# Chunk tables of a graph kernel: every second batch of step matrices on ScalarE, and PE's expansion loop in turns of 16 groups instead of 64

## The reference

```python
def _spmm(row, col, vals, x):
    msg = vals[:, None] * x[col]
    return segment_sum(msg, row, num_segments=N)
def _layer(x_prev, row, col, vals, W_a, b_a, W_b, b_b):
    h = _spmm(row, col, vals, x_prev)
    z = (h + x_prev) @ W_a.T + b_a + h * x_prev @ W_b.T + b_b
    return where(z >= 0, z, 0.2 * z)
x = emb[x_ids]; x1 = _layer(x, ...); x2 = _layer(x1, ...); x3 = _layer(x2, ...)
return concatenate((x, x1, x2, x3), axis=1)
```

## Time and profile before

| | us |
|---|---|
| median of 3 runs (8888.81 to 8897.76) | 8891.55 |
| the profiled execution | 8889.35 |
| its span | 8887.5 |
| mean granted TensorE clock, share of full speed | 0.938 |
| busy PE / PEld / DVE | 7889.6 / 7229.6 / 7142.9 |
| busy ACT / POOL | 4541.7 / 5736.8 |

### The profile page before, as it was taken

How to read it: one execution, slowest core, us unless ns; L and a number is a source line. 1 busy time by engine, 2 the same in 40 slices (tenths; PEclk the granted TensorE clock), 3 DMA queues, 4 the chain that set the end, 5 groups by cost and what they waited for, 6 DMA issues and landing times.

```text
span 8887.5 us, 265258 instructions
## 1 busy us (share of the span) xinstructions
PE 7889.6 (89%) x82756; PEld 7229.6 (81%) x82757; DVE 7142.9 (80%) x9830; ACT 4541.7 (51%) x14097; POOL 5736.8 (65%) x4886
## 2 busy tenths in 40 slices
PE   5999995799996688899999788899999788899999
PEld 4777775577774588789999788899999688799999
DVE  8999988799997877777777777777777777777777
ACT  0999990799995366621112566611112566611112
POOL 4787874588883244478886344478885444488884
PEclk8999995899997799999999899999999899999999
DMA  2111111211111488788887588888886688888885
GB/s 79 7 7 7 7 7 39 34 7 7 7 7 26 159 295 294 289 286 283 286 286 244 204 296 295 302 277 286 286 286 220 228 295 290 296 283 286 286 286 199
DMA packets 877540, 1680.36 MB, mean 189 GB/s; under 512 B 262122, under 2 KB 313399, under 8 KB 876404
## 3 DMA queue, kind: packets, MB, share of 16 engines
q0 software_dynamic: 364832, 907.43, 34.4%
q1 hardware_dynamic: 499692, 758.75, 24.0%
q10 hardware_dynamic: 12520, 6.40, 0.2%
HBM read 912.31 MB, written 759.79 MB: 188 GB/s over the span
## 4 chain that ended last, share of the span: by engine, by line
PE 45%; ACT 19%; issue 12%; DMA 8%; SPq 7%; DVE 5%; POOL 1%; ACTq 1%; DVEq 0%; POOLq 0%
PE ps L1037 35%; ACT hT L723 17%; DMA messages<-work 7%; SPq L684 6%; PE ps L1028 5%; PE ps L864 1%; DVE hT L1348 1%; SPq L669 1%; DVE hT L1134 1%; PE ps L1065 1%; PE ps L1045 1%; PE ps L1066 1%; PE ps L891 1%; POOL work L575 1%; DVE work L1385 1%
## 5 line engine op out<-in xcount | busy, mean ns | idle before, releaser
L1037 PE MATMUL ps<-work 128*128 128x125 f32 x26880 | 3111.5, 278 | 52.6 <-DVE work L1414 52.6
L1037 PEld LDWEIGHTS ps<-work 128*128 128x128 f32 x26880 | 3066.2, 192 | 97.9 <-DVE work L1414 57.4
L603 POOL DMA_INDIRECT work<-messages,work x1680 | 2567.6, 1528 | 557.7 <-issue 550.0
L1028 PE MATMUL ps<-xb,work 125*128 x10752 | 1992.4, 226 | 450.9 <-DVE work L1385 265.8
L792 ACT ACTIVATE work<-ps,work 128x128 f32<-128x128 f32 x5376 | 1526.9, 371 | 1073.4 <-PE ps L1028 572.0
L1414 DVE TENSOR_TENSOR work<-work,iota_p 128x1000 f32<-128x1000 f32 x1680 | 2005.2, 1194 | 1.0 <-ACT work L810 0.4
L1028 PE MATMUL ps<-hT,work 125*128 x10752 | 1991.7, 224 | 0.4
L1028 PE MATMUL ps<-work 125*128 x10752 | 1976.6, 224 | 0.8
L810 ACT ACTIVATE work<-work 128x8 f32<-128x8 f32 x1680 | 516.2, 307 | 2527.8 <-DMA work<-messages,work 2527.8
L917 PEld LDWEIGHTS ps<-hT 128*128 128x128 f32 x12768 | 1484.1, 196 | 297.1 <-ACT stage L712 227.9
L917 PE MATMUL ps<-hT 128*128 128x96 f32 x12768 | 1520.1, 280 | 186.6 <-ACT stage L712 186.5
(11 more groups left out here) (212 smaller groups left out, 6096.0 us busy)
## 6 DMA issues: line engine op xcount, KB each, us to landing
messages<-work SPq DMA_DIRECT2D x2688, 258.0 KB, 4.0
work<-messages,work POOLq DMA_INDIRECT x1680, 5.9
out_x<-xb SPq DMA_DIRECT2D x150, 125.0 KB
sorted_edges<-stage,run_idx POOLq DMA_INDIRECT x798
work<-slot_cols SPq DMA_DIRECT2D x672, 4.0 KB
work<-lane_places SPq DMA_DIRECT2D x532, 5.2 KB, 2.1
out_x<-xb ACTq DMA_DIRECT2D x4, 1562.5 KB
sorted_edges<-hT SPq DMA_DIRECT2D x4, 908.0 KB
```

The costliest lines, as they stand in the source:

```text
L603: pool.indirect_dma_start(out=ck[:, n, :, :].rearrange("p j e -> p (j e)"), out_offset=None, in_=messages, in_offset=bass.IndirectOffsetOn ...
L1028: last = t.matmul(ps[:, n % PR, j * D:(j + 1) * D], col_hot[:, at:at + P], piece[:, bass.ds(offset, D)], start=k == 0, stop=k == 2)
L1037: last = t.matmul(part[n], ck[:, n, j, 0:D], sel[:, n % SELB, j, :], start=j == 0, stop=j == CHB - 1)
```

## The change

Two parts of the kernel are changed, and the rest stands as it was.

In the chunk tables, the batches with odd numbers are made by ScalarE. It takes Sign(x + 0.5 - tt[1]), which is 1 where the comparison is true and -1 where it is not, one tile per instruction. For these tiles the differences are multiplied by 0.5 ahead, and the sum lacks a constant, half of the sum of all differences, which is SLOTS2 / 2 and is added behind the reduction. There are four buffers instead of two, a semaphore for each of the two makers, and one more table, tt[5], with 0.5 - tt[1].

In the expansion, PE's loop does 16 groups per turn, 56 turns in a layer. At the head of a turn it loads 16 bytes into 16 registers; each holds one block number, and there is no shift and no mask.

```diff
-LB = 4
-CQ = 2
+CQ = 4
-        group_at = wi[0:1, TBL0 + 2 * TB:TBL0 + 2 * TB + GROUPS // 4]
-        group_bytes = wu[0:1, 4 * (TBL0 + 2 * TB):4 * (TBL0 + 2 * TB) + GROUPS]
+        group_at = wu[0:1, 4 * (TBL0 + 2 * TB):4 * (TBL0 + 2 * TB) + GROUPS]
...
+            act.wait_ge(vals_kept, GPP)
+            act.wait_ge(starts_ready, 1)
+            for k in range(1, TB // CR, 2):
+                act.wait_ge(cstep_used, k + 1)
+                for n in range(CR):
+                    last = s.activation(chunk_step[:, k % CQ, n, :], iota_p[0:NBD, :], ACT.Sign, bias=tt[5][:, k * CR + n:k * CR + n + 1])
+                last.then_inc(cstep_ready[1], 1)
...
             for k in range(TB // CR):
-                pe.wait_ge(cstep_ready, k + 1)
+                pe.wait_ge(cstep_ready[k % 2], k // 2 + 1)
...
-                with pe.Fori(0, ABODIES // LB) as i:
-                    _, four = nc.values_load_multi_w_load_instructions(
-                        group_at[0:1, bass.ds(i * (LB * AU // 4), LB * AU // 4)], engines=[mybir.EngineType.PE],
-                        min_val=0, max_val=(NB - 1) * 0x01010101,
-                        skip_runtime_bounds_check_because="the table holds four numbers of blocks in each word")
-                    for n in range(LB * AU):
-                        offset = ((four[n // 4] >> (n % 4 * 8)) & 255) * D
-                        offset.max_val = (NB - 1) * D
+                with pe.Fori(0, ABODIES) as i:
+                    _, block_of = nc.values_load_multi_w_load_instructions(
+                        group_at[0:1, bass.ds(i * AU, AU)], engines=[mybir.EngineType.PE],
+                        min_val=0, max_val=NB - 1, skip_runtime_bounds_check_because="the table holds numbers of blocks")
+                    for n in range(AU):
...
-                                                piece[:, bass.ds(offset, D)], start=k == 0, stop=k == 2)
+                                                piece[:, bass.ds(block_of[n] * D, D)], start=k == 0, stop=k == 2)
...
+            signed = delta_t.rearrange("c (b e r) h -> c e b (r h)", e=2, r=CR)[:, 1, :, :]
+            link(v.tensor_scalar(signed, signed, 0.5, None, ALU.mult))
+            v.tensor_scalar(tt[5], tt[1], -1.0, 0.5, ALU.mult, ALU.add).then_inc(starts_ready, 1)
-            for k in range(TB // CR):
+            for k in range(0, TB // CR, 2):
                 dve.wait_ge(cstep_used, k + 1)
                 v.tensor_tensor(chunk_step[:, k % CQ, :, :], iota_p[0:NBD, :][:, None, :].to_broadcast([NBD, CR, P]),
                                 tt[1][:, k * CR:(k + 1) * CR][:, :, None].to_broadcast([NBD, CR, P]),
-                                ALU.is_ge).then_inc(cstep_ready, 1)
+                                ALU.is_ge).then_inc(cstep_ready[0], 1)
...
+            by_sign = chunk_idx.rearrange("p (b e r) -> p e b r", e=2, r=CR)[:, 1, :, :]
+            link(v.tensor_scalar(by_sign, by_sign, SLOTS2 / 2, None, ALU.add))
```

More of the change, by code:

```diff
@@ L263, in graph_layers @@
         base_of = work[:, TBL0 + TB:TBL0 + 2 * TB]
-        group_at = wi[0:1, TBL0 + 2 * TB:TBL0 + 2 * TB + GROUPS // 4]
-        group_bytes = wu[0:1, 4 * (TBL0 + 2 * TB):4 * (TBL0 + 2 * TB) + GROUPS]
-        assert ABODIES % LB == 0 and NB <= 128
+        group_at = wu[0:1, 4 * (TBL0 + 2 * TB):4 * (TBL0 + 2 * TB) + GROUPS]
+        assert 4 * TBL0 % 16 == 0 and TB % 2 == 0 and AU % 16 == 0 and NB <= 256
         row_at = wi[0:1, TBL0 + 2 * TB + GROUPS:TBL0 + 3 * TB + GROUPS]
@@ L283, in graph_layers @@
         TT0 = 18 * NBD + max(TBW, GTW) * NB
-        tt = [hT[0:NBD, TT0 + k * TB:TT0 + (k + 1) * TB] for k in range(5)]
-        TS0 = TT0 + 5 * TB
+        tt = [hT[0:NBD, TT0 + k * TB:TT0 + (k + 1) * TB] for k in range(6)]
+        TS0 = TT0 + 6 * TB
         chunk_step = hb[0:NBD, 2 * TS0:2 * TS0 + CQ * CR * P].rearrange("c (q r x) -> c q r x", q=CQ, r=CR)
         delta_t = hb[0:NBD, 2 * (TS0 + CQ * CR * P // 2):2 * (TS0 + CQ * CR * P // 2) + 3 * TB].rearrange("c (t h) -> c t h", h=3)
-        assert TB // 4 * 3 <= 512 and TB % (4 * CR * CQ) == 0 and TS0 + CQ * CR * P // 2 + 2 * TB <= HSORT
+        assert TB // 4 * 3 <= 512 and TB % (4 * CR) == 0 and TS0 + CQ * CR * P // 2 + 2 * TB <= HSORT
         part = [ps[:, n, 0:BLK] for n in range(BU)]
@@ L354, in graph_layers @@
         tabs_done = sem("tabs_done")
-        cstep_ready = sem("cstep_ready")
+        starts_ready = sem("starts_ready")
+        cstep_ready = [sem(f"cstep_ready{e}") for e in range(2)]
         cstep_used = sem("cstep_used")
@@ L658, in _ @@
             sp.wait_ge(offsets_stored, 3 * DMA)
-            sp.dma_start(group_bytes, group_blocks.rearrange("p t -> (p t)")[0:GROUPS].rearrange("(a t) -> a t", a=1)).then_inc(offsets_in, DMA)
+            sp.dma_start(group_at, group_blocks.rearrange("p t -> (p t)")[0:GROUPS].rearrange("(a t) -> a t", a=1)).then_inc(offsets_in, DMA)
             sp.dma_start(row_at, tile_rows.rearrange("p t -> (p t)")[0:TB].rearrange("(a t) -> a t", a=1)).then_inc(offsets_in, DMA)
@@ L1013, in _ @@
                 pe.sem_inc(pe_layers, 1)
-                with pe.Fori(0, ABODIES // LB) as i:
-                    _, four = nc.values_load_multi_w_load_instructions(
-                        group_at[0:1, bass.ds(i * (LB * AU // 4), LB * AU // 4)], engines=[mybir.EngineType.PE],
-                        min_val=0, max_val=(NB - 1) * 0x01010101,
-                        skip_runtime_bounds_check_because="the table holds four numbers of blocks in each word")
-                    for n in range(LB * AU):
-                        offset = ((four[n // 4] >> (n % 4 * 8)) & 255) * D
-                        offset.max_val = (NB - 1) * D
+                with pe.Fori(0, ABODIES) as i:
[3 more added lines that the diff above has]
+                    for n in range(AU):
                         if n % 2 == 0:
-                            pe.wait_ge(col_hot_ready, la * (GROUPS // 2) + i * (LB * AU // 2) + (n // 2 + 1))
-                        pe.wait_ge(msg_ready[n % 2], la * (GROUPS // 2) + i * (LB * AU // 2) + (n // 2 + 1))
+                            pe.wait_ge(col_hot_ready, la * (GROUPS // 2) + i * (AU // 2) + (n // 2 + 1))
+                        pe.wait_ge(msg_ready[n % 2], la * (GROUPS // 2) + i * (AU // 2) + (n // 2 + 1))
                         for j in range(CH):
```

## The result

The changed kernel takes 9671.81 us (median of 4, 9669.28 to 9674.77) against 8894.65 us (4 runs of the kernel before). The ratio is 1.087, with a 95% interval of 1.085 to 1.089: 777 us slower. The prediction said 8805 us, 8675 to 8890, and gave slower a chance of 0.13. The profiled execution took 9673.08 us with a span of 9671.3.

A forecast was written before the change was run, and what follows sets the result against it. DVE bounds the chunk tables; in the expansion, message stores bound most of a turn and PE the time around each gap. From 8889.35 us, 17.6 (tables) and 67.1 (loop) come off: 8804.6, said as 8805 us, range 8675 to 8890.

The forecast's parts named there:

- The tables: Chunk-table loop: odd batches on ScalarE make it the new bound, 85.4 us against 103.0, a gain of 17.6 us.
- The lower bound of the gain: Chunk tables: worst case, no overlap between ScalarE's activations, 109 us for them, gain put at -9 us.
- The branch: End of a turn of PE's expansion loop: with 384 records the branch falls from 4.19 to 0.21 us.
- the rule of two pages: PE's loop branch: a target outside two 256-instruction blocks stalls for a fetch, so the branch stays long; chance 0.04.
- Nothing shows that bytes are quicker, so 1.76: Head of PE's expansion turn: loading 16 bytes into 16 registers takes 1.76 us, as 16 words did.
- six of ten: PE's gaps in the expansion loop: the clock falls at six gaps of ten, costing 1.0 us per 16 groups.
- rival 3: PE's expansion loop: the branch stays long, 6.1 us idle per 16 groups, 19.7 us in all, 9733 us; chance 0.04.
- The rest of the sum: Expansion per 16 groups: matmuls 11.1, PE idle 2.1, clock 1.0 us; with the stores' slack 14.1 us.
- Rival 1: Expansion: message stores become the bound, by a short byte load or a held clock, 13.3 us per 16 groups, 8672 us; chance 0.20.

The follow-up runs named there:

- eight-word run: Changed kernel with 32 groups per turn of PE's expansion loop and block numbers packed four to a word, eight words loaded per turn: 8679.76 us, ratio 0.975.
- run with 16 words: Changed kernel with block numbers as 16 words of 32 bits, one per group, instead of 16 bytes; same turn of 16 groups: 8738.21 us, ratio 0.982.
- four-word: Changed kernel with 16 groups per turn, but block numbers packed four to a word, four words loaded per turn, shifted and masked: 8682.9 us, ratio 0.975.
- kernel with four bytes a load: Changed kernel with its 16 bytes in four loads of four, each ahead of its four groups: 8897.86 us in one run.

## Why the prediction was wrong

**The tables were right.** 17.6 us forecast, 19.5 measured in the trace. The lower bound of the gain was given as -9 us; by its own terms it is -8. ScalarE is the bound with 280 activations from 2848.68 to 2930.1, 0.292 us apart (taken 0.297). The scaling of the differences took 0.39 us instead of some 0.85, and four buffers were enough: the activations never waited. No second table load is seen.

**The branch was right.** I gave the rule of two pages a chance of 0.04 and took 0.21 us by the nearest row; it was 0.213. The eight-word run goes further: 768 records and still 0.213 us, which no window of two pages of 256 instructions holds. By the rule of the two-page window in the Trainium skill (Runtime: NRT & Kernel Launch, "Instruction fetch mechanics") both would be slow; the measurement decides against it. In these loops the limit for PE lies between 768 and 1536 records a turn.

**The step that failed** is "Nothing shows that bytes are quicker, so 1.76", with its bounds of 1.1 to 2.2 us. It measured 6.26 us. With it PE's idle time was 6.05 us a turn in the median, not 2.1, and the clock fell at every one, not at six of ten, so 192 matmuls took 13.1 us and not 12.1: 19.2 us per 16 groups in place of 14.1. The row was one of 16 words, and I carried it over by the number of registers, looking only for a reason why bytes would be quicker and none why they would be slower. An element's width was a change of form that no row of before showed, and the bounds had to be wider above than the spread of the old form. The same section of the Trainium skill ("Instruction fetch mechanics") has a figure that spoke for a longer load: about 200 ns per register, given for register loads from HBM, where these read SBUF. For 16 words, which would be 3.2 us, the trace is well under it (1.1 us at least, 1.76 in the median); for 16 bytes the least, 3.78 us or 0.24 us each, is near it, and the median of 6.26 us is above. By that figure of the Trainium skill the load would have been 3.2 us, an estimate; that is 1.4 us more in each gap, 15.5 us per 16 groups, and a forecast of slower.

**The time of rival 3 came true by another cause.** It priced 6.1 us of PE idle for each 16 groups at 19.7 us, and 19.2 were measured, with the load in the place of the branch: that price was of the idle time and not of what made it, and that the two times lie so close is luck. Its chance of 0.04 was that of the branch alone; the ways to the same idle time were not added up.

**The rest of the sum, tested by the run with 16 words.** I had PE at 11.1 us of matmuls, 2.1 us idle and 1.0 us for the clock, with 1.76 us of load. There the load was 2.13 us, the idle time 1.9 us in the median, and the result 13.65 us per 16 groups, so the sum was some 0.4 us too high. Its granted clock of 0.96 over 500 us, 37 turns, puts the clock's price at about 0.04 x 500 / 37 = 0.54 us a turn: the fall, taken at six idle times of ten and found at 53 of 165, was the term that was too large. Rival 1, the stores as the bound at 13.3 us and 8672 us, is what the four-word and eight-word runs are: 13.27 us, 8683 and 8680 us.

## What to carry to other kernels

Price a register load by the form of its elements: narrow ones cost some three times a word apiece (6.26 against 2.13 us for sixteen), so pack them into words and let the sequencer shift and mask. When a loop's turn is cut shorter, whatever stands once per turn must be cut in the same measure; where no row shows the form of an instruction, its price needs a bound on both sides. An idle time of one engine is harmless until the buffers behind it run dry: here 0.8 us at the head of a turn cost nothing (four words) and 6 us cost a third of the stage.

## What the runs showed of the hardware

Register loads on PE, the least of each row: one word 0.30 us, four 0.33, eight 0.59, sixteen 1.1; four bytes 0.98, sixteen bytes 3.78, sixteen halfwords 3.79. From 8 to 16 that is 0.065 us a word, from 4 to 16 it is 0.23 us a byte. Where I looked, the least loads of four elements and more are those with the DMA engines almost still, whatever the compute engines do: a load of four bytes took 0.98 us at a DMA share of 0.04, with PE, DVE and ACT at work, and another 1.71 us at 0.77. Not every load at a high share is long: four words took 0.36 to 0.69 us with the share at 1. Over all turns the medians are 0.31, 0.59, 1.01 and 2.13 us for words, 1.23 and 6.26 us for bytes, 6.24 us for halfwords.

The granted clock fell behind 53 of 165 idle times of 1.9 us in the median (sixteen words), behind all 165 of some 6 us (sixteen bytes), and behind none in the kernel with four bytes a load, whose idle times are 0.3 to 1.4 us. What the sequencer does differently for narrow elements stays open. The limit between a branch that refetches and one that does not was not looked for more closely.
